# Rotating q and k by a second set of projected columns, with the low part on VectorE and the shift in bf16, in one attention stage of a two-layer decoder

## The reference, cut to what matters

```python
def frac_rope(x):                       # the last axis is 128 wide
    rot, skip = jnp.split(x, 2, axis=-1)        # 64 rotated, 64 untouched
    even, odd = jnp.split(rot, 2, axis=-1)      # 32 and 32
    r_even = even * cos - odd * sin
    r_odd = even * sin + odd * cos
    return jnp.concatenate([r_even, r_odd, skip], axis=-1)
q, k, v = x @ wq, x @ wk, x @ wv        # per head
q = frac_rope(q) * 128 ** (-0.5)
k = frac_rope(k) * 128 ** (-0.5)
s = q @ k.T, masked to the keys up to the query
out = softmax(s) @ v @ wo               # then added to x and layer-normalised
```

## Time and profile before

| | |
|---|---|
| device time, median of 3 runs | 3536.33 us (3522.80 to 3537.49) |
| the profiled execution, its own time | 3536.33 us |
| its span in the trace | 3534.6 us |
| PE busy | 3155.5 us, 89% of the span |
| DVE busy | 2376.1 us, 67% |
| ACT busy | 1705.0 us, 48% |
| POOL busy | 1732.3 us, 49% |
| the stage touched | about 2346 to 2612 us of the span |

### The profile page before, as it was taken

The page is one execution under the profiler, slowest core; times in us unless marked ns, Lnnn a source line. Parts: engine busy times, 40 slices in busy tenths (PEclk is TensorE's granted clock), DMA queues, the critical chain, the costliest instruction groups (busy, mean ns, idle before and its releaser), DMA issues. The chain is left out here.

```text
span 3534.6 us, 63848 instructions
## 1 busy us (share of the span) xinstructions
PE 3155.5 (89%) x24201; PEld 1817.3 (51%) x24201; DVE 2376.1 (67%) x5271; ACT 1705.0 (48%) x2086; POOL 1732.3 (49%) x1163
## 2 busy tenths in 40 slices
PE   6799999989999999999999962868979999999797
PEld 3566666654555555555555522755644434444346
DVE  5899999964556655655655646146427978888528
ACT  1688888852444344434434441223222766666641
POOL 2788888833777777777777830223460000000012
PEclk9899999999999999999999976988986999999898
DMA  2100000011000000000000043720021111111101
GB/s 59 38 2 2 2 2 2 2 27 28 4 1 4 1 4 1 3 4 1 4 1 1 1 149 111 235 66 1 1 41 18 18 18 17 18 17 18 32 1 36
DMA packets 61305, 87.31 MB, mean 25 GB/s; under 512 B 9457, under 2 KB 51314, under 8 KB 60146
## 3 DMA queue, kind: packets, MB, share of 16 engines
q1 hardware_dynamic: 57970, 79.22, 9.3%
q0 software_dynamic: 3072, 4.34, 0.7%
HBM read 60.24 MB, written 8.54 MB: 19 GB/s over the span
## 5 line engine op out<-in xcount | busy, mean ns | idle before, releaser
L921 DVE TENSOR_REDUCE x0hm<-x0pM 128x1 f32<-128x400 f32 (+1 forms) x1024 | 520.3, 561 | 379.9 <-PE x0pM L823 379.9
L402 POOL TENSOR_SCALAR rows<-rows,mb 128x1024 bf16<-128x1024 bf16 x512 | 567.4, 1119 | 145.9 <-DVE mb L354 145.9
L348 DVE TENSOR_SCALAR_CACHE_REDUCE rows<-pS 128x1024 bf16<-128x1024 f32 x512 | 616.5, 1205 | 19.1 <-PE pS L297 19.1
L413 ACT ACTIVATE prT<-pP 128x1024 bf16<-128x1024 bf16 x512 | 523.3, 1024 | 134.5 <-PE pP L308 134.1
L1387 DVE TENSOR_REDUCE x1hm<-x1pM 128x1 f32<-128x400 f32 (+1 forms) x1024 | 519.5, 566 | 90.9 <-PE x1pM L1273 87.8
L1506 ACT ACTIVATE x1pr<-x1pST 128x1024 f32<-128x1024 f32 (+1 forms) x416 | 403.8, 1022 | 200.8 <-PE x1pST L1325 200.7
L783 POOL TENSOR_TENSOR x0acc<-x0acc,x0pr 128x1024 f32<-128x1024 f32 (+1 forms) x176 | 421.6, 2395 | 110.9 <-ACT x0pr L1032 95.2
L783 POOL TENSOR_TENSOR x0acc<-x0acc,o_nat 128x1024 f32<-128x1024 f32 (+1 forms) x176 | 419.0, 2381 | 72.0 <-ACT o_nat L1032 53.2
L1273 PE MATMUL x1pM<-x1sk,x1sq 64*128 64x400 f32 (+1 forms) x1024 | 322.4, 446 | 29.3 <-DMA x1sq<-x1ql 13.7
L1032 ACT ACTIVATE o_nat<-x0pST 128x1024 f32<-128x1024 f32 (+1 forms) x208 | 212.9, 1024 | 279.9 <-PE x0pST L867 279.4
L1032 ACT ACTIVATE x0pr<-x0pST 128x1024 f32<-128x1024 f32 (+1 forms) x208 | 212.9, 1024 | 279.5 <-PE x0pST L867 279.5
(11 more groups left out here) (364 smaller groups left out, 5179.2 us busy)
## 6 DMA issues: line engine op xcount, KB each, us to landing
m_w<-in_moe_w1T SPq DMA_DIRECT2D x16, 1024.0 KB, 9.9
m_w<-in_moe_w2T SPq DMA_DIRECT2D x16, 1024.0 KB, 6.9
x1sq<-x1qh SPq DMA_DIRECT2D x32, 128.0 KB, 4.5
x1sk<-x1kh SPq DMA_DIRECT2D x32, 100.1 KB, 3.6
rows_d<-m_xr SPq DMA_DIRECT2D x1, 2176.0 KB, 7.8
acc_d<-m_zero SPq DMA_DIRECT2D x4, 514.0 KB, 7.0
m_acc<-acc_d SPq DMA_DIRECT2D x4, 514.0 KB, 7.2
g_xN<-in_x SPq DMA_DIRECT2D x1, 2048.0 KB, 9.2
```

Source lines behind the costliest of these rows:

```text
L348: nc.vector.tensor_scalar(rows[u][:, half * 1024:(half + 1) * 1024], pS[half][:, :], 1.0, None, ALU.mult, ALU.max, accum_out=mx[u][:, half ...
L402: nc.gpsimd.tensor_scalar(r, r, -1.0, mb[u][:, 0:1], ALU.mult, ALU.add).then_inc(s_df, 1)
L413: nc.scalar.activation(prT[u][:, half * 8:(half + 1) * 8, :], pP[half][:, :, :], ACT.Exp, scale=-1.0 / HD ** 0.5).then_inc(s_ex, 1)
L921: emptied(nc.vector.tensor_reduce(hm[g % 2][:, a, t, i % 8 // 2:i % 8 // 2 + 1], bank(name)[:, 0:w], AX.X, ALU.max, negate=True), name)
```

## The change

The projection gives two further units for each item, `qs` and `ks`: the same projection by a weight matrix whose columns are permuted, so that the bank holds the other half of the rotated pair in each row. The host lays out these two more matrices, and the sines as 128 rows, with signs and with zeros for the untouched half. DVE's rotation becomes `straight` (bank times cosine), `swapped` (second bank times sine, and the sum over 128 rows). The low parts move from POOL to DVE: that of q stands behind `straight` of k, that of k behind `swapped` of k. `tb` becomes one buffer, of 128 rows. The `shift` tile becomes one row of bf16, and the matmul that adds it has one row of weights in bf16; its two zero-fills go. As `ahead[:2]` is now another pair of units (for items 3, 5 and 7 it is q and `qs`), the shift stands before k and `ks` there, and the even deal over steps falls elsewhere.

```diff
@@ project
-        units = [("q", x), ("k", x)]
+        units = [(k, x) for k in ("q", "qs", "k", "ks")]
...
-        cos, sin = m.sb("a1cos", [P, T]), m.sb("a1sin", [HD // 2, T])
-        w = [m.sb(f"a1w{h}", [P, DJ, 2, HD]) for h in range(H)]
+        cos, sin = m.sb("a1cos", [P, T]), m.sb("a1sin", [P, T])
+        w = [m.sb(f"a1w{h}", [P, DJ, 4, HD]) for h in range(H)]
...
-        shift = [m.sb(f"a1shift{i}", [P, QG], F32R) for i in range(2)]
+        shift = [m.sb(f"a1shift{i}", [1, QG], BF16) for i in range(2)]
@@ gpsimd
-                for i in range(2):
-                    nc.gpsimd.memset(shift[i][:, :].bitcast(F32), 0.0).then_inc(s_zero, 1)
...
-                def low(name):
...
-                    nc.gpsimd.tensor_tensor(dst, ta["qk".index(kind)][:, :], high.bitcast(F32), ALU.subtract)\
-                        .then_inc(s_lo, 1)
...
-                    for name in units_in(n):
-                        if name[0] in ("q", "k"):
-                            low(name)
@@ tensor
-                    part = "qk".index(kind)
+                    part = {"q": 0, "qs": 1, "k": 2, "ks": 3}[kind]
...
-                        mm = nc.tensor.matmul(o, G.ones[:, :].bitcast(F32R), shift[x % 2][:, min(column(x, kt), 2 * P):],
+                        mm = nc.tensor.matmul(o, G.ones_b[0:1, :], shift[x % 2][:, min(column(x, kt), 2 * P):],
                                               start=False, stop=True)
@@ vector
-                def rotated(name):
+                def low(kind, x):
+                    g, h = x // H, x % H
+                    here = slice(g * QG, (g + 1) * QG)
+                    dve.wait_ge(s_hi, 2 * x + (1 if kind == "q" else 2))
+                    high = qh[h][g % 2][:, :] if kind == "q" else kh[h][:, here]
+                    dst = ql[h][g % 2][:, :] if kind == "q" else kl[h][:, here]
+                    nc.vector.tensor_tensor(dst, ta["qk".index(kind)][:, :], high.bitcast(F32), ALU.subtract)\
+                        .then_inc(s_lo, 1)
+
+                def straight(name):
                     kind, x = name
                     wait_filled(dve, name)
                     dve.wait_ge(s_rot[x // H], 32)
                     here = slice((x // H) * QG, (x // H + 1) * QG)
...
-                    nc.vector.tensor_tensor(mine[:, :], bank(name)[:, :], cos[:, here], ALU.mult).then_inc(s_cos, 1)
-                    nc.vector.tensor_tensor(swapped[upper, :], bank(name)[lower, :], sin[lower, here], ALU.mult)\
-                        .then_inc(s_sin, 1)
-                    emptied(nc.vector.tensor_tensor(swapped[lower, :], bank(name)[upper, :], sin[upper, here], ALU.mult), name)
...
-                    nc.vector.tensor_tensor(mine[both, :], mine[both, :], swapped[both, :], ALU.add).then_inc(s_add, 1)
+                    emptied(nc.vector.tensor_tensor(ta["qk".index(kind)][:, :], bank(name)[:, :], cos[:, here], ALU.mult),
+                            name)
+                    if kind == "k":
+                        low("q", x)
+
+                def swapped(name):
+                    kind, x = name[0][0], name[1]
+                    wait_filled(dve, name)
+                    here = slice((x // H) * QG, (x // H + 1) * QG)
+                    emptied(nc.vector.tensor_tensor(tb[:, :], bank(name)[:, :], sin[:, here], ALU.mult), name)
+                    wait_emptied(dve, (kind, x))
                     wait_emptied(dve, name)
+                    mine = ta["qk".index(kind)][:, :]
+                    nc.vector.tensor_tensor(mine, mine, tb[:, :], ALU.add).then_inc(s_add, 1)
+                    if kind == "k":
+                        low("k", x)
...
-                    emptied(nc.vector.tensor_copy(shift[x % 2][0:1, :], bank(name)[0:1, :]), name)
+                    emptied(nc.vector.tensor_copy(shift[x % 2][:, :], bank(name)[0:1, :]), name)
@@ rotary_tables, layout
-            np.concatenate([s, -s]))
+            np.concatenate([-s, s, np.zeros((64, T), np.float32)]))
...
+    swap = np.concatenate([np.arange(32, 64), np.arange(0, 32), np.arange(64, 128)])
...
-        "a1_w": np.stack([a1["wq"].reshape(D, D), a1["wk"].reshape(D, D)]),
+        "a1_w": np.stack([a1["wq"].reshape(D, D), a1["wq"][:, :, swap].reshape(D, D),
+                          a1["wk"].reshape(D, D), a1["wk"][:, :, swap].reshape(D, D)]),
```

More of the change, by code:

```diff
@@ L1618, in l1_self_attention @@
         kl = [m.sb(f"a1kl{h}", [P, T], F32R) for h in range(H)]
-        ta, tb = [m.sb(f"a1ta{i}", [P, QG]) for i in range(2)], [m.sb(f"a1tb{i}", [HD // 2, QG]) for i in range(2)]
+        ta, tb = [m.sb(f"a1ta{i}", [P, QG]) for i in range(2)], m.sb("a1tb", [P, QG])
         pr = [m.sb(f"a1pr{i}", [P, 2, QG]) for i in range(NP)]
@@ L1642, in l1_self_attention @@
         s_rot, s_set, s_eps = [m.sem(f"a1_tables{c}") for c in range(NG)], m.sem("a1_masks"), m.sem("a1_epsset")
-        s_zero, s_cos, s_sin, s_add, s_hi, s_lo = m.sem("a1_zeroed"), m.sem("a1_cos"), m.sem("a1_sin"), m.sem("a1_rotated"), m.sem("a1_high"), m.sem("a1_low")
+        s_add, s_hi, s_lo = m.sem("a1_rotated"), m.sem("a1_high"), m.sem("a1_low")
         s_nm, s_st, s_ex, s_pv = (m.sem("a1" + k) for k in ("_negmax", "_scores", "_exp", "_values"))
@@ L1713, in _ @@
                                         base=0, pattern=[[1, P]], channel_multiplier=-1).then_inc(s_set, 1)
-                def low(name):
[L1715 to L1722, removed]
-                    nc.gpsimd.tensor_tensor(dst, ta["qk".index(kind)][:, :], high.bitcast(F32), ALU.subtract)\
-                        .then_inc(s_lo, 1)
-                for name in first:
-                    if name[0] in ("q", "k"):
-                        low(name)
                 for n, (x, u) in enumerate(steps):
@@ L1831, in unit @@
                         pe_.wait_ge(s_free[number[name] % 3], number[name] // 3)
-                    {"q": rotated, "k": rotated, "v": value_rows, "max": maximum,
+                    {"q": rotated, "qs": rotated, "k": rotated, "ks": rotated, "v": value_rows, "max": maximum,
                      "shift": shifts, "sum": total, "out": out, "x": transposes,
@@ L1926, in shifts @@
                     wait_filled(dve, name)
-                    dve.wait_ge(s_zero, 2)
                     if x >= 2:
                         dve.wait_ge(s_st, start[x - 1])
-                    emptied(nc.vector.tensor_copy(shift[x % 2][0:1, :], bank(name)[0:1, :]), name)
+                    emptied(nc.vector.tensor_copy(shift[x % 2][:, :], bank(name)[0:1, :]), name)
                 def total(name):
@@ L1995, in unit @@
                     if name[0] not in ("v", "x", "z"):
-                        {"q": rotated, "k": rotated, "max": maximum, "shift": shifts,
+                        {"q": straight, "qs": swapped, "k": straight, "ks": swapped, "max": maximum, "shift": shifts,
                          "sum": total, "out": out}[name[0]](name)
@@ L2026, in high @@
                 def high(name):
-                    kind, x = name
+                    kind, x = name[0][0], name[1]
                     g, h = x // H, x % H
@@ L2048, in unit @@
                 def unit(name):
-                    if name[0] in ("q", "k"):
+                    if name[0] in ("qs", "ks"):
                         high(name)
```

8 lines of the change are left out of this document (removed).

## The result

The changed kernel took 3582.59 us (median of 4 runs, 3567.90 to 3586.25), the kernel before 3535.98 us beside it. The ratio is 1.0133 with a 95% interval of 1.0095 to 1.0170: slower, by 47 us and not by the 17 forecast, and outside the range. The profiled execution of the changed kernel took 3560.77 us, 24 us more than that of before. So I compare the stage itself, from PE's first transpose in it to the first projection of the next stage.

The account below looks back on a forecast made before the run. PE was taken to set the pace, so added projections count except where they fall into its gaps. Projections +18.9 and bf16 shift -2.2 gave +16.7 us on 3536.3: 3553 us (+0.47%), range 3539 to 3568.

Parts of the forecast that it names:

- the shift matmul in bf16: At the 80 shift matmuls: 0.07 us gained at each of 32 behind a mask, -2.2 us; bounds -8 to +15.
- the exposed loads: Rival: one-row shift matmul exposes weight loads, 0.1 to 0.19 us at each of 80, 3563 to 3570 us; chance 0.13.
- The rival's "against": Argument against exposed weight loads at the one-row shift: loads behind masks in bf16 are not late.
- The projections and DVE, +18.9: Added projections and DVE's chain, followed place by place from the first scores to item 7: together +18.9 us.
- first scores: Ahead of the first scores: longer projections of items 0 and 1, gap still 3.5 us, slow stretch stays, +5.8 us.
- the first rival: Low-clock stretches at item 2 (-3) and behind item 3's gap (-3.4) unsure; one or both: 3547 to 3550 us; chance 0.2.
- Item 3: Item 3's projection: 4.5 us wait closed, a 5 us gap returns one step later behind `expert_rows`; +5.7 us.
- Items 5 and 7: Ends of these projections: gaps close; item 5 -2.9 us with its slow stretch gone, item 7 +1.5 us.
- The low parts on DVE: DVE keeps four operations for each of q and k, low part taken at 0.68 us; k's waits for ACT's high part.
- the 3.0 us chain: DVE behind a filled `ks` bank: product, sum, ACT's high part, low part; 3.0 us, 0.8 of it idle.
- DMA and start: Weight and sine loads at the stage's start each grow by 128 KB: costed at nothing, 0.3 us if sines doubled.
- Number of slow stretches: Low-clock PE stretches after longer gaps; wrong if two or five; none at the end of item 3.

Follow-up runs that it names:

- 128-row kernel: The kernel before with a bf16 shift of 128 rows (zeros below the first) and bf16 ones of 128 rows: stage 271.8 us (-2.2).
- experiment 6: The kernel before with a bf16 shift of 64 rows and ones of 64 rows: stage 298.1 us (+24.1).

## Why the prediction was wrong

The experiments split the 41.9 us by steps in one row: projections alone +10.9 (284.9), new place of the shift -2.7 (282.2), low parts on DVE +6.6 (288.8), one-row shift +27.2 (315.9).

- **The step that failed: the shift matmul in bf16, -2.2.** It measured +27.2 in the changed kernel and +31.0 by itself. I took the saving of the bf16 format from the rows with masks, and that was right: it is the -2.2 us of the 128-row kernel, where a step of two shifts behind masks is 0.14 us shorter and one without masks about the same. But the edit has two parts, and I priced one, since I took matmuls of 128 rows as the nearest rows. I wrote that no matmul of one row is in the trace. That is so, but the trace of the kernel before is full of changes between 64 rows and 128, in other stages, and they show the price. PE in order of time, then the weight loads:

```profile
1433.93 0.35 PE L823 MATMUL x0pM<-x0kh,x0qh 64*128 64x400 f32 x2
1434.21 0.70 PE L793 MATMUL x0pM<-g_xT,x0wq 128*128 128x512 f32 x1
1433.70 0.19 PEld L823 LDWEIGHTS x0pM<-x0kh,x0qh 64*128 64x128 f32 x2
1434.20 0.30 PEld L793 LDWEIGHTS x0pM<-g_xT,x0wq 128*128 128x128 f32 x2 [0.31 <-issue]
```

  Between two matmuls of 64 rows the load is 0.23 us ahead. The load for 128 rows starts with its own matmul, 0.27 us after one of 64 rows and 400 columns, where 400 columns alone take 0.18 (in proportion to 0.23 for 512). The excess is 0.09, and in the first layer 505 matmuls of 128 rows stand 0.32 us after one of 64 rows and 512 bf16 columns (L297 to L308), as in experiment 6. From such rows the two changes around each shift could have been priced, before anything ran, at an estimate of 0.2 us, 16 us for all 80. I kept the exposed loads as a bound and as a rival, with 0.1 to 0.19 us each and a chance of 0.13. The mechanism of that rival is what happened, at 0.29 each without a mask and 0.23 with one, since the loads on both sides are held and the one behind delays a second start. The bound was too low as well: I took one load of 0.19 and not two, and no term for the clock.
- **The rival's "against".** I held against it that loads behind masks in bf16 are not late. The sign of being wrong that belongs to it, a successor 0.3 us or more after the shift without a mask, came true with 0.32. The argument spoke of the format, and the format was never the trouble. I also wrote that this rival passes 0.5% from 0.04 us each; by my own sum, 16.7 against 17.7 us, 0.0125 each was enough.
- **The projections and DVE, +18.9.** With the old shift 288.8 was measured, +14.8. In detail, from the start of the stage: first scores +4.7 for +5.8, item 3 +11.9 for +16.7 by my sum, item 4 +12.0 for +13.8, the end +14.5 for +18.9. The difference is in the clock: the changed kernel with the old shift had no slow stretch at item 2's projection and half of one at the start (14 us at the low level between its first and last scores, 26 before), which was the first rival ("the clock falls less often").
- **Item 3.** The forecast that the closed gap comes back behind `expert_rows` was right. PE stood there for 5.6 us with 5 forecast, 6.0 with the old shift. DVE's chain in the changed kernel, in order of time:

```profile
2402.32 0.69 DVE L1893 TENSOR_TENSOR a1tb<-a1pM,a1sin 128x512 f32<-128x512 f32 x1 [0.43 <-PE a1pM L1741]
2403.12 0.69 DVE L1897 TENSOR_TENSOR a1ta<-a1ta,a1tb 128x512 f32<-128x512 f32 x1
2404.51 0.69 DVE L1876 TENSOR_TENSOR a1kl<-a1ta,a1kh 128x512 fp32r<-128x512 f32 x1 [0.70 <-ACT a1kh L2023]
2405.12 0.16 DVE L1961 TENSOR_SCALAR m_none<-m_acc 128x4 f32<-128x4 f32 x1
...
2410.94 2.79 DVE L1906 TENSOR_REDUCE a1hm<-a1pM 128x1 f32<-128x512 f32 x5
```

  The product starts at 2402.32, the low part at 2404.51, and `expert_rows` at 2405.12: 2.8 us for a chain put at 3.0, of which 0.70 is the wait for ACT, put at 0.8. The maxima start at 2410.94.
- **Items 5 and 7.** The gaps at their ends closed, as forecast.
- **The low parts on DVE.** I gave no term of its own to them; they were in the 3.0 us chain. They measured 6.6 us, which is more than a third of what I had for all of it. The equal count of DVE's operations hid this from the sum.
- **DMA and start.** The stage's first projection starts 2.72 us after the first transpose in both kernels, and no wait on the tables or weights is among PE's in the changed kernel. Right, at nothing.
- **Number of slow stretches.** From the first scores on I had three: there, at item 2's projection and behind `expert_rows`. The changed kernel has these three, of 6.8 us each by the granted clock, and two more of 3.4 us, in items 5 and 7: five, one of my signs of being wrong. With the old shift there are two, of 3.4 and 10.2 us. So the projections leave fewer slow stretches than I had, and the one-row shift adds some.

What remains open: why the granted clock was lower with one row (0.91 and 0.90) than with 64 (0.93) or 97 and 128 (0.94), in kernels whose units stand in the same order. The changed kernel has 0.95 with one row and 0.97 with the old shift. Nothing was run to separate the rows from the short gaps that the held loads make.

## What to carry to other kernels

A matmul is not cheaper for having fewer rows. If it stands in a stream of full-height matmuls, pad it to more than 64 rows, even with zeros, as the kernel before did with 128. In its place 97 rows cost what 128 do, and one row or 64 cost 0.23 to 0.29 us more; that 65 are enough is read from other matmuls of the trace and was not run for this one. Read PE by the distance from start to start, with the weight loads beside it; the listed durations hid all of this loss. And when one edit changes two properties, price each by its own rows, and look for them in the whole trace and not in the stage alone; where it has none for one of them, measure that first.

A gap on PE can be filled, but what DVE owes behind it comes due at the next bank. Closing it paid for items 5 and 7 and not where `expert_rows` stood behind it.

## What the runs showed of the hardware that I had not expected

- A weight load starts ahead of its matmul, while another runs, if both have 65 to 128 rows (128 beside 65, 96 and 97, and 96 beside 97, in these traces), and if both have 64. Between 64 rows or one and full height it is held, before the matmul and behind it (0.32 and 0.32 us in place of 0.23 for 512 columns). One and 64 are the only low counts compared.
- With one row in the float32 format the successor comes after 0.42 us, 0.10 later than in bf16.
- The first 25 us of the program vary by some 15 us between executions. DVE's first two operations there, of 512 columns, take 18.3 to 18.8 us in seven of the fourteen profiled executions and 1.7 to 3.5 in the others, while POOL's zero-fills of `qT` and `kT` run. DVE in order of time, in the kernel before:

```profile
5.42 18.72 DVE L172 TENSOR_SCALAR xc<-xp,cw 128x512 f32<-128x512 f32 x2 [5.42 <-DMA cw<-in_conv]
```

  in the changed kernel:

```profile
5.23 1.76 DVE L172 TENSOR_SCALAR xc<-xp,cw 128x512 f32<-128x512 f32 x2 [5.23 <-DMA cw<-in_conv]
```

  and POOL beside it, in the changed kernel:

```profile
1.63 15.69 POOL L162 MEMSET qT<- 128x1024 f32 x16
17.26 7.72 POOL L164 MEMSET kT<- 128x1024 f32 x8
```

  In the kernel before DVE's pair ended at 24.1 us, as POOL's fills did (23.3); in the changed one both ran side by side. I didn't try to bring either about, and the cause is not shown. PE's first matmul starts at 27.0 us in the first case and at 12.1 in the second. This is most of why the two profiled executions differ by 24 us and their stages by 42, and why stages are better compared than spans. What it does to the medians is not shown, as those executions left no trace.
